# Feature stage of a vision tower on Trainium2: the GpSimd subtraction moves to the Vector engine, and the last 512 columns of each band are multiplied in float32

## What is computed

```python
xb = 2.0 * jnp.pi * xyz[..., None] * freq_bands        # 6 bands
feat = jnp.concatenate([jnp.sin(xb), jnp.cos(xb)], axis=-1)
feat = feat.reshape(b, n, -1)                           # 576 * 12 features
h = jnp.einsum('bnf,of->bno', feat, W)                  # 512 tokens x 192
```

## Time and profile before

| what | us |
|---|---|
| median of 3 runs | 5643.05 |
| profiled execution | 5627.77 |
| its span | 5626.0 |
| feature stage (to the end of the last `tokens`) | 1390.11 |
| busy over the span: PE / DVE / ACT / POOL | 4651.3 / 4007.4 / 3109.6 / 837.1 |

### The profile page before, as it was taken

The page is one execution under the profiler, slowest core; times in us unless marked ns, Lnnn a source line. Parts: engine busy times, 40 slices in busy tenths (PEclk is TensorE's granted clock), DMA queues, the critical chain, the costliest instruction groups (busy, mean ns, idle before and its releaser), DMA issues. The chain is left out here.

```text
span 5626.0 us, 198571 instructions
## 1 busy us (share of the span) xinstructions
PE 4651.3 (83%) x84786; PEld 3606.0 (64%) x84787; DVE 4007.4 (71%) x8485; ACT 3109.6 (55%) x4426; POOL 837.1 (15%) x394
## 2 busy tenths in 40 slices
PE   4667766766859999999999999999999469699960
PEld 3445544544428888888888888888888335477740
DVE  8889889886536777777777777777787644355545
ACT  4566666664335666665666666666665323277740
POOL 2444444443000000000000000000000013300027
PEclk9888888888879999999999999999999676699985
DMA  1000000000320000000000000000000222222223
GB/s 57 25 25 13 25 25 13 25 25 17 103 49 14 15 21 15 21 15 15 21 15 21 15 21 15 20 16 15 21 15 9 82 66 76 86 68 69 65 63 109
DMA packets 186921, 198.18 MB, mean 35 GB/s; under 512 B 86848, under 2 KB 167040, under 8 KB 183552
## 3 DMA queue, kind: packets, MB, share of 16 engines
q1 hardware_dynamic: 173824, 160.79, 9.6%
q0 software_dynamic: 12288, 25.18, 1.5%
HBM read 123.00 MB, written 62.91 MB: 33 GB/s over the span
## 5 line engine op out<-in xcount | busy, mean ns | idle before, releaser
L643 PE MATMUL y_ps<-k_sb,x_sb 128*12 128x256 f16 x58368 | 1705.6, 275 | 21.5 <-DVE x_sb L880 13.0
L643 PEld LDWEIGHTS y_ps<-k_sb,x_sb 128*12 128x12 bf16 x58368 | 1433.4, 88 | 209.9 <-issue 38.7
L257 PE MATMUL acc<-w_hl,feat_h 128*128 128x384 f16 x3456 | 642.0, 350 | 424.5 <-DVE h_sb L203 299.3
L762 ACT ACTIVATE y_sb<-y_ps 128x256 f32<-128x256 f32 x912 | 347.6, 381 | 920.9 <-PE y_ps L643 920.9
L257 PEld LDWEIGHTS acc<-w_hl,feat_h 128*128 128x128 f16 x3456 | 356.1, 104 | 685.6 <-issue 370.3
L150 POOL TENSOR_TENSOR feat_l<-work,feat_h 128x2048 f16<-128x2048 f32 x96 | 576.3, 6003 | 778.5 <-ACT feat_h L241 739.8
L771 ACT ACTIVATE k_new<-cos,k_bias 128x512 f32<-128x512 f32 x768 | 520.3, 682 | 166.5 <-PE cos L670 166.4
L653 PEld LDWEIGHTS turned_x<-rows_in,y_sb 128*128 128x128 f32 x3648 | 478.1, 191 | 118.9 <-issue 71.6
L911 DVE CUSTOM_DVE_ANT_0 plan<-plan,u_rows,v_last 128x512 f32<-128x512 f32 x768 | 535.2, 744 | 4.1
L653 PE MATMUL turned_x<-rows_in,y_sb 128*128 128x16 f32 x3648 | 527.0, 258 | 8.6 <-ACT y_sb L762 8.4
L241 ACT ACTIVATE feat_h<-work 128x4096 f16<-128x4096 f32 x96 | 388.2, 4044 | 201.5 <-PE acc L264 199.4
(11 more groups left out here) (253 smaller groups left out, 7286.5 us busy)
## 6 DMA issues: line engine op xcount, KB each, us to landing
xt<-in_x_dram SPq DMA_DIRECT2D x16, 1280.0 KB, 5.8
x_in_sb<-expert_rows SPq DMA_DIRECT2D x39, 384.0 KB, 3.2
expert_results<-y_sb SPq DMA_DIRECT2D x39, 384.0 KB, 2.5
q_left<-q_parts SPq DMA_DIRECT2D x192, 64.0 KB, 2.9
q_right<-q_parts SPq DMA_DIRECT2D x192, 64.0 KB, 2.9
v_parts<-v_sb SPq DMA_DIRECT2D x16, 408.0 KB, 2.4
v_in_sb<-v_parts SPq DMA_DIRECT2D x48, 136.0 KB, 3.3
h_tokens<-h_sb SPq DMA_DIRECT2D x16, 384.0 KB, 2.5
```

Of the source, the lines that this page charges most:

```text
L257: nc.tensor.matmul(acc[a][:, q, 0:2 * DIM], block_of, w_hl[:, k, :, :].rearrange("p a d -> p (a d)"), start=(k == 0), stop=False)
L643: last = nc.tensor.matmul(y[a][32 * c:32 * c + XW, :, :], high[:, j, XW * h:XW * (h + 1)], k_sb[s][:, h, :, at:at + P], start=(h == 0 and ...
```

## The change

In the feature stage:

- POOL does no subtraction any more. DVE's `lows` makes the leftovers of sine and cosine in one instruction.
- The last 512 columns of each band (block 3 of an even band, the shared fifth block of an odd one) are not split. PE multiplies them in float32, straight from `waves`, with float32 weights. `feat_h` and `feat_l` hold only the first 1536 or 2048 columns (`SPLIT`).
- The float32 weights of these blocks, `w_full`, take the room of the two float16 parts in `w_hl`, and two further scalings (x 2 instructions in the preparation) write them.
- A new semaphore `waves_used`, raised by PE behind a band's float32 matmuls, joins those that ACT waits for before it writes the next sines there.
- PE's program has images 0 and 1 written out with no wait for h, and a loop of 7 rounds over the rest, in which image i+2 waits for h of image i.

```diff
+        SPLIT = [(FULL + n - 1) * TOKENS for n in range(2)]
+        feat_h = [sb(f"feat_h{i}", [P, 2, SPLIT[i]], F16) for i in range(2)]
+        feat_l = [sb(f"feat_l{i}", [P, 2, SPLIT[i]], F16) for i in range(2)]
...
+        per_pair = 2 * (2 * FULL + 1)
+        w_full = w_hl[:, :, :, :].rearrange("p c a d -> p (c a d)").bitcast(F32).rearrange("p (c d) -> p c d", c=NCH)
...
-            with pool.Fori(0, IMAGES) as i:
-                for b in range(BANDS):
-                    n, hi = b % 2, (FULL + b % 2) * TOKENS
-                    pool.wait_ge(high_ready[n], START + i * UNITS + (b // 2 + 1))
-                    pool.wait_ge(feat_used[n], START + i * UNITS + b // 2)
-                    nc.gpsimd.tensor_tensor(feat_l[n][:, 1, 0:hi], waves[n][:, 1, 0:hi], feat_h[n][:, 1, 0:hi],
-                                            ALU.subtract).then_inc(low_cos_ready[n], 1)
...
+            for c in (2 * FULL - 2, per_pair - 2):
+                done(nc.vector.tensor_scalar(w_full.rearrange("p (u c) d -> p u c d", c=per_pair)[:, :, c:c + 2, :],
+                                             raw.rearrange("p (u c) d -> p u c d", c=per_pair)[:, :, c:c + 2, :],
+                                             scale[:, 0:1], None, ALU.mult))
...
-                nc.vector.tensor_tensor(feat_l[n][:, 0, 0:hi], waves[n][:, 0, 0:hi], feat_h[n][:, 0, 0:hi],
-                                        ALU.subtract).then_inc(low_sin_ready[n], 1)
+                nc.vector.tensor_tensor(feat_l[n][:, :, :], waves[n][:, :, 0:SPLIT[n]], feat_h[n][:, :, :],
+                                        ALU.subtract).then_inc(low_ready[n], 1)
...
-                    act.wait_ge(low_sin_ready[n], START + i * UNITS + b // 2)
-                    act.wait_ge(low_cos_ready[n], START + i * UNITS + b // 2)
+                    act.wait_ge(low_ready[n], START + i * UNITS + b // 2)
+                    act.wait_ge(waves_used[n], START + i * UNITS + b // 2)
...
-                    nc.scalar.activation(feat_h[n][:, :, 0:hi], waves[n][:, :, 0:hi], ACT.Copy).then_inc(high_ready[n], 1)
+                    nc.scalar.activation(feat_h[n][:, :, :], waves[n][:, :, 0:SPLIT[n]], ACT.Copy).then_inc(high_ready[n], 1)
...
+            def image(i, a):
+                for b in range(BANDS):
+                    n = b % 2
+                    chunks = [(2 * k + t, s, t) for k, (band, s) in enumerate(CHUNKS) if band == b for t in range(2)]
+                    halved = [(k, s, t) for k, s, t in chunks if (s + 1) * TOKENS <= SPLIT[n]]
+                    pe.wait_ge(high_ready[n], START + i * UNITS + (b // 2 + 1))
+                    for k, s, t in halved:
+                        for q in range(TB):
+                            block_of = feat_h[n][:, t, s * TOKENS + q * P:s * TOKENS + (q + 1) * P]
+                            nc.tensor.matmul(acc[a][:, q, 0:2 * DIM], block_of, w_hl[:, k, :, :].rearrange("p a d -> p (a d)"),
+                                             start=(k == 0), stop=False)
+                    for k, s, t in chunks[len(halved):]:
+                        for q in range(TB):
+                            block_of = waves[n][:, t, s * TOKENS + q * P:s * TOKENS + (q + 1) * P]
+                            last = nc.tensor.matmul(acc[a][:, q, 0:DIM], block_of, w_full[:, k, :], start=False, stop=False)
+                    last.then_inc(waves_used[n], 1)
+                    pe.wait_ge(low_ready[n], START + i * UNITS + (b // 2 + 1))
+                    for k, s, t in halved:
+                        for q in range(TB):
+                            block_of = feat_l[n][:, t, s * TOKENS + q * P:s * TOKENS + (q + 1) * P]
+                            last = nc.tensor.matmul(acc[a][:, q, 0:DIM], block_of, w_hl[:, k, 0, :],
+                                                    start=False, stop=(b == BANDS - 1 and k == halved[-1][0]))
+                    last.then_inc(feat_used[n], 1)
+
+            image(0, 0)
+            image(1, 1)
+            with pe.Fori(0, IMAGES // 2 - 1) as pair:
                 for a in range(2):
...
+                    pe.wait_ge(h_ready, START + pair * 2 + (a + 1))
+                    image(pair * 2 + (a + 2), a)
```

More of the change, by code:

```diff
@@ L85, in embed @@
         waves = [work[:, (4 + 2 * i) * WIDE:(6 + 2 * i) * WIDE].rearrange("p (t n) -> p t n", t=2) for i in range(2)]
-        feat_h = [sb(f"feat_h{i}", [P, 2, WIDE], F16) for i in range(2)]
-        feat_l = [sb(f"feat_l{i}", [P, 2, WIDE], F16) for i in range(2)]
+        SPLIT = [(FULL + n - 1) * TOKENS for n in range(2)]
+        feat_h = [sb(f"feat_h{i}", [P, 2, SPLIT[i]], F16) for i in range(2)]
+        feat_l = [sb(f"feat_l{i}", [P, 2, SPLIT[i]], F16) for i in range(2)]
         w_hl = sb("w_hl", [P, NCH, 2, DIM], F16)
+        per_pair = 2 * (2 * FULL + 1)
+        w_full = w_hl[:, :, :, :].rearrange("p c a d -> p (c a d)").bitcast(F32).rearrange("p (c d) -> p c d", c=NCH)
         wabs = sb("wabs", [P, 1], F32)
@@ L106, in embed @@
         high_ready = [sem(f"high_ready{i}") for i in range(2)]
-        low_sin_ready = [sem(f"low_sin_ready{i}") for i in range(2)]
-        low_cos_ready = [sem(f"low_cos_ready{i}") for i in range(2)]
+        low_ready = [sem(f"low_ready{i}") for i in range(2)]
+        waves_used = [sem(f"waves_used{i}") for i in range(2)]
         feat_used = [sem(f"feat_used{i}") for i in range(2)]
@@ L187, in angles, with lows @@
                                         ALU.bitwise_and).then_inc(turns_ready[n], 1)
-            def low_sines(i, b):
-                n, hi = b % 2, (FULL + b % 2) * TOKENS
+            def lows(i, b):
+                n = b % 2
                 dve.wait_ge(high_ready[n], START + i * UNITS + (b // 2 + 1))
                 dve.wait_ge(feat_used[n], START + i * UNITS + b // 2)
-                nc.vector.tensor_tensor(feat_l[n][:, 0, 0:hi], waves[n][:, 0, 0:hi], feat_h[n][:, 0, 0:hi],
-                                        ALU.subtract).then_inc(low_sin_ready[n], 1)
+                nc.vector.tensor_tensor(feat_l[n][:, :, :], waves[n][:, :, 0:SPLIT[n]], feat_h[n][:, :, :],
+                                        ALU.subtract).then_inc(low_ready[n], 1)
             def tokens(i, a):
@@ L212, in image @@
                         angles(i + 1, 1 - a, 0)
-                    low_sines(i, b)
+                    lows(i, b)
                     if before and b == 1:
@@ L245, in _ @@
             pe.wait_ge(w_ready, START + 1)
-            with pe.Fori(0, IMAGES // 2) as pair:
-                for a in range(2):
[L248 to L259, removed]
-                        pe.wait_ge(low_cos_ready[n], START + i * UNITS + (b // 2 + 1))
-                        for k, s, t in chunks:
-                            for q in range(TB):
-                                block_of = feat_l[n][:, t, s * TOKENS + q * P:s * TOKENS + (q + 1) * P]
-                                last = nc.tensor.matmul(acc[a][:, q, 0:DIM], block_of, w_hl[:, k, 0, :],
-                                                        start=False, stop=(k == NCH - 1))
-                        last.then_inc(feat_used[n], 1)
```

## The result

The changed kernel takes 5266.06 us (median of 4 runs, 5258.01 to 5274.43), the kernel before 5643.73 us. The ratio is 0.9331, with a 95% interval of 0.9313 to 0.9349. It is faster by 378 us where the forecast had 259, and outside the range of 5370 to 5458. The profiled execution took 5258.01 us, its span is 5256.2 us.

What follows compares the result with a forecast made beforehand. PE was to bound the changed feature stage: 61.0 + 16 x 66.2 + 1.5 + 7 + 2.1 = 1130.8 us against 1390.1, 259 less, giving 5384 us; range 5370 to 5458.

Steps and rivals of the forecast that it cites:

- What bounds the kernel now: Feature stage before: no engine full; PE waits 20 us per image for h, and POOL's subtractions stretch DVE's instructions.
- DVE without POOL: Feature stage: DVE keeps undisturbed durations, leftovers 3.37 and 4.45 us, 59.1 us an image with the tokens instructions.
- The float32 matmul: PE, feature stage: 0.520 us each, from the projection behind the attention; 48 add 25.0 us, making 66.2 us an image.
- The four passes: PE's float32 matmul: true FP32 as four array passes would be cheaper than the trace's 0.520 us; the trace row decides.
- The wait for h: PE at each image's head: the 20 us per image go and nothing takes their place.
- ACT's new wait: ACT waits on waves_used before the next sines: 4 us to spare in the tight odd band, so PE runs without gap.
- Start: Feature stage's start: scalings 0.6 us each, 1.7 added with hand-offs; PE starts at 61.0, low clock adds 1.5 us.
- The loop's edge: PE's feature loop: edge now bare, 0 to 3.1 us seven times; 1 each taken, 7 us in all.
- D: Rival on PE: float32 at four passes, 0.33 us, PE 57.0 us, DVE's 59.1 the bound, 5278 us; chance 0.04.
- A: Rival on PE: losses where float32 runs begin and end, plus loop's edge, 70.9 us an image, 5452 us; chance 0.14.
- B: Rival on PE: clock drops in float32 runs, 0.937 us a matmul, 19.9 us more an image, 5702 us; chance 0.08.

Runs made afterwards that it cites:

- p1: Kernel before with only PE's new program order (images 0 and 1 written out, image i+2 waits for h of image i): 5607.25 us, ratio 0.9949.
- p6: Kernel before with the float32 part alone, POOL still subtracting the cosine half and the old wait kept: 5577.99 us, ratio 0.9855.
- e2: Changed kernel, float32 sine and cosine matmuls of the same tokens in succession, cosine blocks cut to 64 rows so 128 and 64 alternate: 5369.8 us.
- e3: Changed kernel, float32 sine and cosine matmuls of the same tokens in succession, both cut to 64 rows: 5271.26 us.
- e4: Changed kernel with 128-row and 64-row float32 matmuls grouped in the projections and router behind the feature stage: 5211.98 us, ratio 0.9238.

## Why the prediction was wrong, point by point

- **What bounds the kernel now.** Right. The wait at PE's head and POOL's lock on DVE are shown by `p1` to `p6`.
- **DVE without POOL.** Right within 0.02 us an instruction, and 58.9 for 59.1 us an image.
- **The float32 matmul: the step that failed.** "I take 0.520, since PE will have next to no idle time": it measured 0.324. I took the two projections as the bounds, of the same shape and at either clock, but both paid for a thing that the changed stage doesn't have. The working itself names it ("takes turns with one of 64 rows that keeps the same pace"): I read the equal pace as a sign that the rows don't matter, where it was the turns that cost, as `e2` and `e3` show. With 0.324, PE's work is 41.2 + 15.6 = 56.8 us an image, below DVE's 59.1. So the forecast period was 7.3 us too long and the wrong engine was the bound: 16 x 7.3 = 117 of the 126 us by which the stage ended earlier than forecast.
- **The four passes.** By the Trainium skill (FP8 and Floating Point Precision, TensorE Precision Notes) true FP32 is four passes. Four times the measured 0.0825 us is 0.330, and the trace has 0.324: the time is that of four passes, and my row was the exception. I let the row decide without asking why it was dearer than passes by 0.19 us.
- **The wait for h.** Right: it goes, and nothing takes its place.
- **ACT's new wait.** Right that it doesn't bound: ACT waited for PE's float32 part 7 us in all.
- **Start.** The two scalings took 2.07 us, and PE began at 62.07 instead of 61.0 us. Its first 24 matmuls took 6.84 us (to 68.91) where 3.90 is the full pace, so 2.9 us were lost and not 1.5.
- **The loop's edge.** 7 us taken, none found there. But the written-out images lengthened a later loop's edge by 15 us, which no term covered.
- **Rivals.** What came is D, with 0.04: DVE-bound, 5278 forecast, 5266 measured. Its mechanism is right; that its number is only 12 us off is partly luck. D's sum ends the stage at 1025.2 us, and it ended at 1005.1: 11 us for hand-offs that weren't there, 7 for a loop's edge that wasn't, and small terms. Against these 20 us stand the 15 that the stages behind lost, which no term had, and the median lay 8 us above the profiled execution, not 15. A (seams): float16 and float32 runs meet without a gap. B (clock): 1.00 throughout. The range left D out because its chance was set by one row.

## What to carry to other kernels

When two rows price the same operation, ask what stands beside it there, not only whether shape and clock agree; a price that no count of passes explains is paid for something else. A change that takes one of two coupled causes away shows little alone (0.5% for the head), so cost such parts together. And where POOL and DVE read the same memory, an instruction handed to POOL can cost DVE more than doing it itself.

## What the runs showed of the hardware

- Float32 matmuls whose stationary operand alternates between 128 and 64 rows cost 0.18 to 0.20 us more each than a run with equal rows (`e2`, `e4`, the projection of the earlier trace rows). From float16 matmuls of 128 rows into a float32 run of 64 rows the change cost 0.20 us, and back out of it 0.10 (`e3`).
- Runs of float32 matmuls at 0.324 us between float16 ones left the granted clock at 1.00 from 69 us to the end of the feature stage.
- A float32 matmul shows as two records, each of 0.162 us for 192 columns.
- A loop's edge on PE stood bare for 0 to 4.5 us. Sinkhorn's 13 gaps summed to 37 to 39 us in the five kernels with no image written out ahead of the feature loop, and to 49 to 53 us in the eleven with two.
